# Norm weights applied to turned rows, and the openings of four phases reordered, in a two-layer cross-attention kernel

## The chip, the cores and the metric

The kernel runs as one program on one core of a Trainium2 chip. The metric is device time in microseconds (us); three timed runs of the kernel before had a median of 3099.26 us (3098.64 to 3100.08).

## The reference, cut to what matters

Sixteen sequences of 256 rows with 512 channels pass through two layers; sixteen heads of 32 channels each. The first layer normalises x and the context (each with its own gain and shift), attends under a given mask, adds, and runs an MLP of 2048 hidden channels with GELU. The second layer does a causal self-attention without norm in front, a norm, a cross-attention to the context, a norm (ln2), a small MLP with ReLU, and a last norm.

```
xq  = layer_norm(x, qn_w, qn_b);  ctx = layer_norm(context, cn_w, cn_b)
x   = x + softmax(mask(xq @ q_w, ctx @ k_w)) @ (ctx @ v_w) @ proj_w + proj_b
x   = x + gelu(layer_norm(x, n2_w, n2_b) @ fc1_w + fc1_b) @ fc2_w + fc2_b
x1  = layer_norm(x + mha(x, x, causal), ln1_g, ln1_b)
x2  = layer_norm(x1 + mha(x1, context), ln2_g, ln2_b)
out = layer_norm(x2 + relu(x2 @ f1.T + f1_b) @ f2.T + f2_b, ln3_g, ln3_b)
```

In the second layer each head's keys count only up to a length, which is the number of scores of its row 0 that are not zero, and rows of x that are all zero are masked.

## The kernel before

There are four phases, each with its own buffers, semaphores and a barrier at its end: masked attention (tiles named `mask_`, 0 to 729 us in the trace), the MLP (`mlp_`, 733 to about 1525), causal attention (`causal_`, 1530 to 2150) and cross-attention with the small MLP (`cross_`, 2154 to the end). A phase hands its rows to the next through DRAM. Nothing of a phase starts before the barrier.

Each number is kept as a high part that TensorE takes whole (type fp32r) and a low part, the rest. A product is therefore three matmuls for each block of 128 inputs (`product`, L99): high by high, high by low, low by high. High parts are made by ScalarE (matrix_hi at L462 and L464, `turned` at L470), low parts by VectorE as a difference (matrix_lo at L780, `turned` at L820, `qk_lo` at L830 and L835).

The order of work is written out by hand, engine by engine, in functions `mask_turn`, `causal_turn` and `cross_turn`, one turn for each sequence, 16 turns in a phase; the middle ones run as a hardware loop. In a turn TensorE interleaves, for sequence b, scores (L1279), the turning of exponentials (`turn_probs`, L1300) and products with values (L1319), and, for b+1, the turning of the rows (`turn_over`, L1227) and their products with the matrices. In the cross phase the ln2 norm of sequence b-1 and its MLP lie in the same turn (L1337 turns the normed rows). Engines wait by counted semaphores. In the MLP a turn has 512 rows and 16 steps m; step m is `hidden(m)` and `down(m-1)`, 12 matmuls of 128x512 each, and at the end of a turn TensorE turns the next rows (L2035).

Before its first turn each phase has an opening: rows are loaded by SyncE's DMA queue, matrices of 1 MB each (512x512) arrive through two staging slots, and a slot is loaded again only when both parts of what it held are made. The MLP has eight such pieces, four of W1 and then four of W2; all eight are made before the first rows are normed (`apply`, L1958) and turned.

In the mask phase and in the MLP the norm's gain is folded into the matrix (ScalarE's scale at L462 and L1915), and the norm's shift is sent through the unscaled matrix once as a bias: matmuls with one column, L1205 and L2024, and L1210 for the values. In the cross phase gain and shift of ln2 are applied to the rows before they are turned, by `ln_gain` (L916) and `ln_shift` (L925), two instructions each on VectorE.

## Time and profile before

| | before |
|---|---|
| median of 3 timed runs | 3099.26 us |
| the profiled execution | 3095.5 us, span 3093.7 us |
| mean granted TensorE clock | 0.962 |
| busy: TensorE (PE) | 2857.9 us, 92% |
| busy: VectorE (DVE) | 1759.6 us, 57% |
| busy: ScalarE (ACT) | 1614.8 us, 52% |
| busy: GpSimd (POOL) | 566.5 us, 18% |

Busy time is the time in which an engine had an instruction running. A clock of 1.0 is 2.4 GHz and 0.5 is 1.2 GHz. The profiled execution lies 3.8 us under the median of the timed runs, and its span lies 1.8 us under its own time. In the rows further down, `[25.57 <-DVE mlp_xn L1958]` behind an instruction says that its engine had been idle for 25.57 us until that instruction of VectorE released it; "x8" says that eight were merged in one row.

### The profile page before, as it was taken

The numbers are of one execution on the slowest core, as the hardware profiler recorded it, in microseconds if no ns is written. First come the engines' busy times: TensorE is split into PE (matmuls) and PEld (weight loads), VectorE is DVE, ScalarE is ACT, GpSimd is POOL, SyncE is SP. The second block draws the span as 40 slices with busy tenths as digits, with TensorE's granted clock in tenths as the row PEclk, the third lists the DMA queues.
The fourth block names the chain that finished last, engine by engine and source line by source line (L and its number), as shares of the span: only waits on it lengthen the run. The fifth ranks groups of instructions, "written<-read, shape, count | busy, mean of one in ns | idle before, by whom it ended". The sixth has DMA issues, their size and how long they took to land. (4 is left out here: it accounts for less than half of the span.)

```text
span 3093.7 us, 69198 instructions
## 1 busy us (share of the span) xinstructions
PE 2857.9 (92%) x25032; PEld 2480.7 (80%) x25032; DVE 1759.6 (57%) x5398; ACT 1614.8 (52%) x4889; POOL 566.5 (18%) x709
## 2 busy tenths in 40 slices
PE   7999999996699999999789999995799999999995
PEld 6888888885588888888688888884688888888884
DVE  5666666663333323323267777774576767667674
ACT  4777777773211111111167777775565665656662
POOL 1110111110000000000012222333021313223132
PEclk9999999997799999999899999997899999999997
DMA  2111111113100000000111111112201111100100
GB/s 93 45 56 56 56 49 35 55 42 107 54 28 27 14 14 27 27 27 14 61 36 55 41 41 41 41 41 76 93 28 41 41 41 41 40 34 34 41 28 21
DMA packets 73746, 134.35 MB, mean 43 GB/s; under 512 B 9040, under 2 KB 9040, under 8 KB 73680
## 3 DMA queue, kind: packets, MB, share of 16 engines
q1 hardware_dynamic: 73680, 133.47, 12.6%
q8 instruction: 41, 0.67, 0.1%
q14 instruction: 25, 0.20, 0.0%
HBM read 99.90 MB, written 33.55 MB: 43 GB/s over the span
## 5 line engine op out<-in xcount | busy, mean ns | idle before, releaser
L1926 ACT ACTIVATE mlp_h<-mlp_f,mlp_hb 128x512 f32<-128x512 f32 x128 | 88.3, 690 | 579.8 <-PE mlp_f L99 579.8
L1969 DVE CAST mlp_hT_hi<-mlp_h 128x512 fp32r<-128x512 f32 x128 | 58.1, 454 | 471.6 <-ACT mlp_h L1926 471.6
L888 DVE CUSTOM_DVE_ANT_0 mask_scores<-mask_scores,mask_mask 128x256 f32<-128x256 f32 x512 | 201.6, 457 | 93.8 <-PE mask_scores L1279 93.8
L502 ACT ACTIVATE mask_prob<-mask_scores,mask_low 128x256 f32<-128x256 f32 x512 | 237.4, 476 | 22.5 <-DVE mask_low L888 22.5
L502 ACT ACTIVATE cross_prob<-cross_scores,cross_low 128x256 f32<-128x256 f32 x512 | 238.0, 493 | 6.7 <-DVE cross_low L882 6.7
L502 ACT ACTIVATE causal_prob<-causal_scores,causal_low 128x128 f32<-128x128 f32 (+1 forms) x512 | 211.5, 434 | 13.2 <-DVE causal_low L888 13.1
L99 PE MATMUL mlp_f<-mlp_xT_hi,mlp_w_hi 128*128 128x512 f32 x512 | 200.4, 391 | 1.5 <-DVE mlp_xT_lo L1963 1.5
L99 PE MATMUL mlp_f<-mlp_xT_hi,mlp_w_lo 128*128 128x512 f32 x512 | 200.1, 391 | 0.0
L99 PE MATMUL mlp_f<-mlp_xT_lo,mlp_w_hi 128*128 128x512 f32 x512 | 200.1, 391 | 0.0
L2049 PE MATMUL mlp_acc<-mlp_w_hi,mlp_hT_hi 128*128 128x512 f32 x512 | 199.9, 390 | 0.0
L2049 PE MATMUL mlp_acc<-mlp_w_hi,mlp_hT_lo 128*128 128x512 f32 x512 | 199.3, 389 | 0.0
L2049 PE MATMUL mlp_acc<-mlp_w_lo,mlp_hT_hi 128*128 128x512 f32 x512 | 199.2, 389 | 0.0
L888 DVE CUSTOM_DVE_ANT_0 causal_scores<-causal_scores,causal_tri 128x128 f32<-128x128 f32 (+1 forms) x512 | 164.7, 395 | 30.2 <-PE causal_scores L1285 30.2
L364 POOL TENSOR_SCALAR cross_q<-cross_own_head,cross_qk_parts 128x128 fp32r<-128x128 f32 x128 | 69.2, 552 | 605.5 <-DVE cross_qk_parts L835 605.5
L99 PE MATMUL causal_work<-causal_xT_hi,causal_w_hi 128*128 128x256 f32 x512 | 159.2, 311 | 16.7 <-DVE causal_xT_lo L820 16.7
L882 DVE TENSOR_REDUCE cross_low<-cross_scores 128x2 f32<-128x512 f32 x256 | 160.1, 683 | 18.1 <-PE cross_scores L1285 17.5
L99 PE MATMUL causal_work<-causal_xT_hi,causal_w_lo 128*128 128x256 f32 x512 | 145.5, 284 | 0.0
L99 PE MATMUL causal_work<-causal_xT_lo,causal_w_hi 128*128 128x256 f32 x512 | 145.0, 283 | 0.0
L514 ACT ACTIVATE cross_probT<-cross_probsT 128x512 f32<-128x512 f32 x128 | 76.4, 597 | 128.1 <-PE cross_probsT L1300 128.1
L364 POOL TENSOR_SCALAR causal_q<-causal_own_head,causal_qk_parts 128x128 fp32r<-128x128 f32 x128 | 58.0, 465 | 361.1 <-DVE causal_qk_parts L835 361.1
L99 PEld LDWEIGHTS causal_work<-causal_xT_hi,causal_w_hi 128*128 128x128 f32 x512 | 97.7, 191 | 29.2 <-issue 29.2
L514 ACT ACTIVATE mask_probT<-mask_probsT 128x512 f32<-128x512 f32 x128 | 76.7, 599 | 76.2 <-PE mask_probsT L1300 76.2
(313 smaller groups left out, 9327.3 us busy)
## 6 DMA issues: line engine op xcount, KB each, us to landing
mask_x_in<-in_x SPq DMA_DIRECT2D x16, 512.0 KB, 4.0
mask_c_in<-in_ctx SPq DMA_DIRECT2D x16, 512.0 KB, 5.2
mask_res<-in_x SPq DMA_DIRECT2D x16, 512.0 KB, 3.7
after_attention<-mask_res SPq DMA_DIRECT2D x16, 512.0 KB, 5.9
mlp_x<-after_attention SPq DMA_DIRECT2D x8, 1024.0 KB, 5.6
after_layer<-mlp_y SPq DMA_DIRECT2D x8, 1024.0 KB, 4.2
causal_x_in<-after_layer SPq DMA_DIRECT2D x16, 512.0 KB, 3.6
causal_res<-after_layer SPq DMA_DIRECT2D x16, 512.0 KB, 3.9
```

Of the source, the lines that this page charges most:

```text
L99: last = pe.matmul(out, lhs(k, a), rhs(k, c), start=(k == 0 and n == 0), stop=(k == KC - 1 and n == len(PASSES) - 1))
L364: ins = pool.tensor_scalar(Q0[:, part, :], own_head[:], QK[:, c % 2, 1 - part, 0:1].bitcast(F32), 1.0, ALU.mult, ALU.mult)
L502: ins = act.activation(prob[:, u % 4, qt, 0:w], SC[h][:, FROM[qt]:FROM[qt] + w], ACT.Exp, bias=low[:, u % 4, qt:qt + 1], scale=-1.0, accum ...
L514: act.activation(probT[:, u % 8, 0:n], PT_BANK[u % HC][:, 0:n], ACT.Copy).then_inc(s["copied"], 1)
L882: ins = dve.tensor_reduce(low[:, u % 4, :], SC[h][:].rearrange("p (t k) -> p t k", t=TT), AX_X, ALU.min)
L888: ins = dve.tensor_tensor_reduce(SC[h][:, at], SC[h][:, at], extra, 1.0, F32_MAX, ALU.add, ALU.min, low[:, u % 4, qt:qt + 1])
L1926: act.activation(h32[:, m % 2, :], F1[m % 2][:], ACT.Gelu, bias=hb[:, m:m + 1]).then_inc(s["gelu"], 1)
L1969: dve.tensor_copy(hT[0][:, r, :], h32[:, r, :]).then_inc(s["h_hi"], 1)
L2049: ins = pe.matmul(ACC[t][:], hT[a][:, m % 2, t * P:(t + 1) * P], W2[p][:, m, :], start=(m == 0 and n == 0), stop=(m == MH - 1 and n == 2))
```

## The change

Mask phase: matrices are no longer scaled and no bias is computed. Instead ScalarE applies gain and shift while it copies turned rows out of PSUM, two instructions of 128x256 into a new tile `t32`, and VectorE makes the high part by a copy and the low part by a difference, both from `t32`. The copy of q and k becomes one ScalarE instruction of 512 columns and one VectorE instruction, before two each. The copy of the values moves from VectorE to ScalarE. TensorE waits for ScalarE only (`t_act`) before it writes the bank of scores again.

All three attention phases: the first rows' DMA is followed at once by all matrices, each with its own staging place (in `probT` and `prob`, which are free then); high and low parts are made in the order in which TensorE takes them, and signalled for each block of 128 inputs; `first_product` waits block by block.

MLP: rows first, then pieces alternately from W1 and W2 through two own staging slots; `apply` and the first turning follow the first piece, and the other pieces are made during turn 0. Gain and shift are applied to turned rows as above. In every later turn `turn_over` of the next rows is split: two before `down(14)`, two before `down(15)`.

Causal phase: `front` and `rows_seen`, the scan of the next rows for zeros, move on VectorE from behind `ln_var` to behind `minima(b, 3)`.

Cross phase: `ln_gain` and `ln_shift` become `normed_rows`, two instructions behind `cuts(b, 2)`; the gain goes into the copies of the turned rows (`post_hi`, `post_lo`, two instructions where one was), the shift goes through fc1 once (`shift_through`, 16 matmuls with one column), and GpSimd applies gain and shift to the residual rows (`residual(b)`, four instructions of 128x512 in each turn, behind `query0(b, 3)`).

```diff
@@ ScalarE, attention phases @@
             def turned(b, k):
                 act.wait_ge(s["t_ps"], NP * b + k + 1)
+                if masked_ctx:
+                    if k >= 2 or not isinstance(b, int) or b > 0:
+                        act.wait_ge(s["t_lo"], NP * b + k - 1)
+                    at = 2 * (k // 2)
+                    for i in range(2):
+                        ch = 2 * (k % 2) + i
+                        ins = act.activation(t32[:, k % 2, i, :], T_BANK[k][:, i * S:(i + 1) * S], ACT.Identity,
+                                             scale=wcol[:, at, ch:ch + 1], bias=wcol[:, at + 1, ch:ch + 1])
+                    ins.then_inc(s["t_act"], 1)
+                    return
@@ VectorE, attention phases @@
-                dve.wait_ge(s["w_hi_done"], i + 1)
...
+                for k in range(KC):
+                    dve.wait_ge(s["w_hi_done"], KC * i + k + 1)
...
+                if masked_ctx:
+                    dve.wait_ge(s["t_act"], NP * b + k + 1)
+                    dve.tensor_copy(dst_t[0][:, sl, :], t32[:, k % 2]).then_inc(s["t_hi"], 1)
+                    dve.wait_ge(s["t_hi"], NP * b + k + 1)
+                    dve.tensor_tensor(dst_t[1][:, sl, :], t32[:, k % 2], dst_t[0][:, sl, :].bitcast(F32), ALU.subtract
+                                      ).then_inc(s["t_lo"], 1)
+                    return
@@ GpSimd, cross phase @@
+            def residual(b):
+
+                hold(pool, s["post_ps"], 2 * b, s)
+                for t in range(TT):
+                    pool.tensor_tensor(res[:, t], res[:, t], g_rep[:], ALU.mult).then_inc(s["res_gained"], 1)
+                for t in range(TT):
+                    pool.wait_ge(s["res_gained"], TT * (b - 1) + t + 1)
+                    ins = pool.tensor_tensor(res[:, t], res[:, t], b_rep[:], ALU.add)
+                ins.then_inc(s["res_shifted"], 1)
@@ TensorE, attention phases @@
+            def first_product(out, i, lhs, rhs, t_lo):
+
+                for k in range(KC):
+                    pe.wait_ge(s["w_lo_done"], KC * i + k + 1)
+                    if k % 2 == 0:
+                        pe.wait_ge(s["t_lo"], t_lo + k // 2 + 1)
+                    for n, (a, c) in enumerate(PASSES):
+                        ins = pe.matmul(out, lhs(k, a), rhs(k, c), start=(k == 0 and n == 0),
+                                        stop=(k == KC - 1 and n == len(PASSES) - 1))
+                return ins
@@ VectorE, MLP @@
             norm(0)
-            for i in range(8):
...
             apply(0)
+            matrix_lo(0)
             for k in range(KC):
                 turned(0, k)
-            with dve.Fori(0, TURNS - 1) as b:
+            matrix_lo(1)
+
+            def turn(b, first=False):
                 for m in range(MH):
                     split(b, m)
+                    if first and m < 6:
+                        matrix_lo(m + 2)
@@ TensorE, MLP @@
                 if not last:
-                    for k in range(KC):
-                        turn_over(b + 1, k)
+                    turn_over(b + 1, 0)
+                    turn_over(b + 1, 1)
+                down(b, MH - 2)
+                if not last:
+                    turn_over(b + 1, 2)
+                    turn_over(b + 1, 3)
                 down(b, MH - 1)
```

VectorE in the MLP's opening, before: these rows stand behind six of the eight pieces' low parts, and end with the first turned rows.

```order
L1993 TENSOR_TENSOR mlp_w_lo<-mlp_xn,mlp_w_hi 128x512 x4
L1993 TENSOR_TENSOR mlp_w_lo<-mlp_y,mlp_w_hi 128x512 x4
L1996 TENSOR_TENSOR mlp_hb<-mlp_f_0,mlp_b1col 128x16
L1958 TENSOR_SCALAR mlp_xn<-mlp_x,mlp_mv,mlp_rstd 128x512 x4
L1963 TENSOR_TENSOR mlp_xT_lo<-mlp_turned,mlp_xT_hi 128x512 x4
```

VectorE in the MLP's opening, changed: the rows from the phase's start to the first turned block.

```order
L1995 BN_STATS mlp_stats<-mlp_x 128x6 x4
L1999 BN_AGGR mlp_mv<-mlp_stats 128x2 x4
L2002 TENSOR_SCALAR mlp_rstd<-mlp_mv 128x4
L2007 TENSOR_SCALAR mlp_xn<-mlp_x,mlp_mv,mlp_rstd 128x512 x4
L2013 TENSOR_TENSOR mlp_w_lo<-mlp_stage,mlp_w_hi 128x512 x4
L2019 CAST mlp_xT_hi<-mlp_xT 128x512
L2021 TENSOR_TENSOR mlp_xT_lo<-mlp_xT,mlp_xT_hi 128x512
```

`apply` (L1958, now L2007) stood behind all eight pieces and now stands ahead of the first one's.

VectorE in a causal turn, before: from the scan of the next rows to the attended rows `causal_z`, which TensorE's `turn_over(b+1, 1)` waits for because it writes the same bank.

```order
L809 TENSOR_REDUCE causal_big<-causal_x_in 128x2
L814 TENSOR_SCALAR causal_m_next<-causal_big 128x2
L843 TENSOR_SCALAR causal_flags,causal_lens<-causal_probsT 128x256
L846 TENSOR_SCALAR causal_cut<-causal_key,causal_lens 128x256
L848 RECIPROCAL causal_nan<-causal_lens 128x1
L850 TENSOR_SCALAR causal_nan<-causal_nan 128x1
L896 RECIPROCAL causal_rs<-causal_sums 128x8
L900 TENSOR_TENSOR causal_rs<-causal_rs,causal_m_cur 128x8
L902 TENSOR_TENSOR causal_z<-causal_attended,causal_rs 128x2x128
```

The same place of the changed kernel.

```order
L870 TENSOR_SCALAR causal_flags,causal_lens<-causal_probsT 128x256
L873 TENSOR_SCALAR causal_cut<-causal_key,causal_lens 128x256
L875 RECIPROCAL causal_nan<-causal_lens 128x1
L877 TENSOR_SCALAR causal_nan<-causal_nan 128x1
L911 RECIPROCAL causal_rs<-causal_sums 128x8
L915 TENSOR_TENSOR causal_rs<-causal_rs,causal_m_cur 128x8
L917 TENSOR_TENSOR causal_z<-causal_attended,causal_rs 128x2x128
```

The scan (L809, L814) is gone from this place.

VectorE in a cross turn, before: from `ln_gain` to the cuts. L52 and L827 are register steps, L923 a wait; L843 starts `cuts`.

```order
L916 SCALAR_TENSOR_TENSOR cross_res<-cross_res,cross_mv,cross_g_rep 128x512 x2
L52 REGISTER_ALU
L827 REGISTER_ALU
L835 TENSOR_TENSOR cross_qk_parts<-cross_work,cross_qk_parts 128x2x256
L923 ISA
L925 SCALAR_TENSOR_TENSOR cross_res<-cross_res,cross_rstd,cross_b_rep 128x512 x2
L843 TENSOR_SCALAR cross_flags,cross_lens<-cross_probsT 128x256
L846 TENSOR_SCALAR cross_cut<-cross_key,cross_lens 128x256
L848 RECIPROCAL cross_nan<-cross_lens 128x1
```

The same place of the changed kernel, from the end of `ln_var` to `normed_rows` (L933).

```order
L926 TENSOR_SCALAR cross_minus_mean<-cross_mv 128x2
L927 TENSOR_SCALAR cross_rstd<-cross_mv 128x2
L861 REGISTER_ALU
L862 TENSOR_TENSOR cross_qk_parts<-cross_work,cross_qk_parts 128x2x256
L870 TENSOR_SCALAR cross_flags,cross_lens<-cross_probsT 128x256
L873 TENSOR_SCALAR cross_cut<-cross_key,cross_lens 128x256
L875 RECIPROCAL cross_nan<-cross_lens 128x1
L52 REGISTER_ALU
L877 TENSOR_SCALAR cross_nan<-cross_nan 128x1
L931 ISA
L933 TENSOR_SCALAR cross_res<-cross_res,cross_minus_mean,cross_rstd 128x512 x2
```

`ln_gain` is gone from ahead of `qk_lo` (L835, now L862), and the norm's instructions stand behind the cuts, not ahead of them.

## Rows read from the trace of the kernel before

**Rows 1.** The page, part 2: TensorE's granted clock in 40 equal slices.
```profile
PEclk9999999997799999999899999997899999999997
```

**Rows 2.** Four openings, two cross turns: us, busy of PE, PEld, DVE, ACT, POOL, clock, DMA.
```profile
0.00:47.60 47.60, 31.28 (x160) 27.71 (x160) 21.15 (x44) 14.04 (x23) 5.76 (x12) 0.96 0.40 141
729.00:803.30 74.30, 31.34 (x144) 30.39 (x145) 32.69 (x51) 22.13 (x37) 7.03 (x8) 0.53 0.45 152
1530.00:1565.50 35.50, 13.70 (x87) 13.23 (x87) 11.97 (x24) 8.73 (x16) 3.66 (x13) 0.58 0.40 134
2154.00:2199.80 45.80, 17.90 (x123) 16.64 (x124) 21.93 (x40) 16.43 (x37) 4.63 (x14) 0.59 0.54 190
2360.80:2414.50 53.70, 51.43 (x519) 45.32 (x518) 37.88 (x89) 32.80 (x102) 14.25 (x19) 1.00 0.11 39
2577.60:2632.30 54.70, 52.61 (x519) 46.77 (x518) 37.86 (x89) 32.80 (x102) 14.24 (x19) 0.97 0.10 38
```

**Rows 3.** TensorE's waits over the run: us in total, times, longest.
```profile
PE mlp_turned L2035 <- DVE mlp_xn L1958: 25.6, 1, 25.6
...
PE cross_scores L1227 <- DVE cross_xT_lo L820: 17.8, 1, 17.8
...
PE cross_scores L1279 <- DVE cross_xT_lo L820: 17.5, 14, 1.3
...
PE causal_attended L1227 <- DVE causal_z L902: 13.3, 14, 1.0
...
PE cross_probsT L1300 <- DVE cross_flags L843: 11.7, 14, 1.5
...
PE mlp_turned L2035 <- DVE mlp_xT_lo L1963: 7.4, 8, 1.0
```

**Rows 4.** Timeline of the mask opening: start us, us, engine, line.
```profile
13.49 6.96 PE L1205 MATMUL mask_work<-mask_wcol,mask_stage 128*128 128x1 f32 x32 [13.49 <-DMA mask_stage<-in_L_xattn_q_w]
...
27.62 5.09 PE L1210 MATMUL mask_work<-mask_stage,mask_bias_rep 128*128 128x512 f32 x8
```

**Rows 5.** Timeline of one mask turn, ScalarE.
```profile
235.40 0.47 ACT L481 ACTIVATE mask_qk_parts<-mask_work,mask_qk_bias 128x256 fp32r<-128x256 f32 x1 [0.19 <-PE mask_work L99]
...
243.57 0.60 ACT L470 ACTIVATE mask_cT_hi<-mask_scores 128x512 fp32r<-128x512 f32 x1 [0.79 <-PE mask_scores L1227]
```

**Rows 6.** Timeline of the MLP opening.
```profile
735.12 0.43 SPq L1856 DMA_DIRECT2D mlp_x<-after_attention  x1
...
741.67 2.47 DVE L1946 BATCH_NORM_STATS2 mlp_stats<-mlp_x 128x6 f32<-128x512 f32 x4 [12.45 <-DMA mlp_x<-after_attention]
...
791.41 5.79 DVE L1958 TENSOR_SCALAR mlp_xn<-mlp_x,mlp_mv,mlp_rstd 128x512 f32<-128x512 f32 x4
...
803.32 0.77 PE L99 MATMUL mlp_f<-mlp_xT_hi,mlp_w_hi 128*128 128x512 f32 x1 [1.50 <-DVE mlp_xT_lo L1963]
```

**Rows 7.** VectorE's groups in the MLP, 900 to 1450 us: busy us, mean ns.
```profile
L1969 DVE CAST mlp_hT_hi<-mlp_h 128x512 fp32r<-128x512 f32 x99 | 45.7, 462 | 352.8 <-ACT mlp_h L1926 352.8
...
L1958 DVE TENSOR_SCALAR mlp_xn<-mlp_x,mlp_mv,mlp_rstd 128x512 f32<-128x512 f32 x24 | 11.5, 542 | 0.0
```

**Rows 8.** Timeline of the causal opening, ScalarE.
```profile
1547.67 2.19 ACT L464 ACTIVATE causal_w_hi<-causal_stage 128x512 fp32r<-128x512 f32 x4 [5.17 <-DMA causal_stage<-in_L_xattn_Wv]
```

**Rows 9.** Timeline of the cross opening, ScalarE.
```profile
2172.45 2.19 ACT L464 ACTIVATE cross_w_hi<-cross_stage 128x512 fp32r<-128x512 f32 x4 [4.84 <-DMA cross_stage<-in_L_xattn_Wv]
```

**Rows 10.** Timeline of one cross turn, VectorE and TensorE.
```profile
2569.20 1.00 DVE L900 TENSOR_TENSOR cross_rs<-cross_rs,cross_m_cur 128x8 f32<-128x8 f32 x1
...
2579.21 1.52 DVE L925 SCALAR_TENSOR_TENSOR cross_res<-cross_res,cross_rstd,cross_b_rep 128x512 f32<-128x512 f32 x2
...
2581.69 1.29 DVE L820 TENSOR_TENSOR cross_xT_lo<-cross_scores,cross_xT_hi 128x512 fp32r<-128x512 f32 x2
...
2583.03 0.63 PE L1279 MATMUL cross_scores<-cross_qk_parts 32*128 32x256 f32 x12 [1.25 <-DVE cross_xT_lo L820]
```

**Rows 11.** TensorE in a stretch of that turn: busy (x), clock.
```profile
2583.60:2587.00 3.40, 3.40 (x36) 0.51 0.00 0
```

More of the change, by code:

```diff
@@ L427, in turn @@
                     query0(b, 3)
+                if prev:
+                    residual(b)
                 if nxt:
@@ L551, in mask_turn @@
                     exps(b, 3)
+                    values(b, 1)
                     copy(b, 0)
@@ L594, in mask_turn @@
                     exps(b, 15)
+                if nxt:
+                    values(b + 1, 0)
+                if cur:
                     copy(b, 12)
@@ L997, in mask_turn @@
                     minima(b, 0, (2, 3))
-                    values(b, 1)
                 if prev:
@@ L1141, in cross_turn @@
                     hidden_parts(b, 1)
+                else:
+                    shift_through()
                 if cur:
@@ L1166, in _ @@
             front(0)
-            if lengths:
-                rows_seen()
-            for i in range(min(NM, 3)):
-                matrix_lo(i)
-            for k in range(NP):
-                turned(0, k)
-            for i in range(3, NM):
-                matrix_lo(i)
-            dve.wait_ge(s["vec_loaded"], IT * NV)
-            if lengths:
-                dve.wait_ge(s["pool_setup"], 4 if causal else 2)
-            qk_lo(0, 0)
-            if masked_ctx:
-                values(0, 0)
-                mask_floats(0)
-            else:
+            if masked_ctx:
+                matrix_lo(0)
+                turned(0, 0)
+                turned(0, 1)
+                matrix_lo(1)
+                turned(0, 2)
+                turned(0, 3)
+                matrix_lo(2)
+                qk_lo(0, 0)
+                mask_floats(0)
+                matrix_lo(3)
+            if causal:
+                rows_seen()
+                turned(0, 0)
+                turned(0, 1)
+                for i in range(NM):
+                    matrix_lo(i)
+                dve.wait_ge(s["pool_setup"], 4)
+                qk_lo(0, 0)
                 cuts(0, 0)
                 qk_lo(0, 1)
+            if cross:
+                rows_seen()
+                turned(0, 0)
+                turned(0, 1)
+                matrix_lo(0)
+                turned(0, 2)
+                turned(0, 3)
+                matrix_lo(1)
+                dve.wait_ge(s["pool_setup"], 2)
+                qk_lo(0, 0)
+                cuts(0, 0)
+                matrix_lo(2)
+                qk_lo(0, 1)
+                matrix_lo(3)
+                matrix_lo(4)
+            dve.wait_ge(s["vec_loaded"], IT * NV)
             turn(0, prev=False)
@@ L1726, in cross_turn @@
                     feed1(b, 1)
+                else:
+                    pe.wait_ge(s["v_ready"], 2 * b + 2)
+                    shift_through()
                 if cur:
@@ L2010, in _ @@
                 finish(b)
+            turn(0, first=True)
+            with dve.Fori(1, TURNS - 1) as b:
+                turn(b)
             for m in range(MH):
@@ L2032, in turn_over @@
                 if k >= 2:
-                    pe.wait_ge(s["t_lo"], KC * b + k - 1)
+                    pe.wait_ge(s["t_act"], KC * b + k - 1)
+                elif first is False:
+                    pe.wait_ge(s["t_act"], KC * b)
                 for t in range(NT):
@@ L2036, in turn_over, with hidden, down @@
                 ins.then_inc(s["t_ps"], 1)
-            def hidden(b, m):
-                product(pe, F1[m % 2][:], lambda k, a: W1[a][:, k, m * P:(m + 1) * P],
-                        lambda k, p: xT[p][:, k, :]).then_inc(s["f1_ps"], 1)
-            def down(b, m):
+            def hidden(b, m, first=False):
+                if first and m % 4 == 0:
+                    pe.wait_ge(s["w_lo"], m // 2 + 1)
+                for k in range(KC):
+                    if m == 0:
+                        pe.wait_ge(s["t_lo"], KC * b + k + 1)
+                    for n, (a, p) in enumerate(PASSES):
+                        ins = pe.matmul(F1[m % 2][:], W1[a][:, k, m * P:(m + 1) * P], xT[p][:, k, :],
+                                        start=(k == 0 and n == 0), stop=(k == KC - 1 and n == 2))
+                ins.then_inc(s["f1_ps"], 1)
+            def down(b, m, first=False):
                 pe.wait_ge(s["h_lo"], MH * b + m + 1)
+                if first and m % 4 == 0:
+                    pe.wait_ge(s["w_lo"], m // 2 + 2)
                 for t in range(NT):
```

372 lines of the change are left out of this document (168 added, 204 removed).

## The prediction

> **What bounds the kernel now.** I read the granted clock over the span first [rows 1]: it is full except at four dips, three where a phase ends and the next opens, and one at the end. The openings measured by themselves [rows 2] say the same: in the MLP's opening TensorE is busy for 31.3 of 74.3 us at a mean clock of 0.53, in the causal one for 13.7 of 35.5 us, in the cross one for 17.9 of 45.8 us. The mask opening has 31.3 of 47.6 us, but much of that is bias matmuls. The last two of those rows are single cross turns, 53.7 and 54.7 us long. So TensorE is the bound inside turns, and nothing but what it waits for can be won there; outside, the order of loads and copies is the bound. The list of TensorE's waits gives the prices [rows 3]: 25.6 us for the normed rows of the MLP, 17.8 us in the cross opening, and in turns four repeated waits: 17.5 and 11.7 us in 14 cross turns each, 13.3 us in 14 causal turns, 7.4 us in eight MLP turnings. No repeated wait of the mask phase is among the large ones.
>
> **MLP opening.** Before, rows land at 741.67, but `apply` runs at 791.41, behind eight pieces, and the first `hidden` begins at 803.32 [rows 6]. Now: the rows' DMA, issued at 735.12 behind four vectors, is first. I put it 1.9 us earlier, so they land at 739.8. Statistics take 2.47, and I allow 2 us for the small steps on VectorE and GpSimd (an estimate): `apply` starts at 744.2. It took 5.79 us beside GpSimd's `residual`, and would take 4 x 0.542 = 2.17 us by the steady rows [rows 7]. `residual(0)` can start at the same time again, so I take 5.8: 750.0. Then the first piece's low parts: a difference of 128x512 is 0.65 us (1.29 for two [rows 10]), four are 2.6: 752.6. Then a copy of 0.46 [rows 7] and a difference of 0.65: the first block is ready at 753.7, and each further one takes 1.1 us, while TensorE needs about 1.3 for its three matmuls at half clock. 803.3 - 753.7 = 49.6 us won. Half clock may hold a little longer, 1.6 us: **-48** (bounds -40 and -53; the first if a late vector or piece holds ScalarE, the second if `apply` runs free of GpSimd). Remaining pieces are made inside turn 0: 2.6 us of VectorE in every 5.5 us step of TensorE, of which `split` takes 1.1; a 1 MB piece at 152 GB/s [rows 2] is 7 us, and two are needed in 22 us. That hides, at a cost of nothing; if it did not, two pieces of stall would be 14 us.
>
> A row and a rule meet in `apply`: the four scalings take 5.79 us beside GpSimd's additions and 2.17 us alone [rows 6, 7]. The Trainium skill, "SBUF — State Buffer", section "Who interferes with whom", says that VectorE in a two-port mode and GpSimd take one port pair in turn for whole instructions, so the loser blocks. By it the opening costs what I took, and with no such lock it would be 3.6 us shorter. It speaks against the new `residual(b)` in the cross phase too, which is the last rival.
>
> **Mask opening.** Two runs of 6.96 us and one of 5.09 leave TensorE: 19.0 us [rows 4]. Not all of it comes back. The first matrix was there at 13.49, behind five vectors; now the vectors come behind x, context and two matrices, that is one further MB, at 141 GB/s [rows 2] 7.4 us later, less 2.3 us because they are not ahead: gain and shift at about 18. From there VectorE has the second matrix's low parts, 2.6, and four turned blocks of 1.1: 25. The K product at half clock is some 2.6 us more, and about 6 us of products lie between it and the first scores in either kernel: 33.6, against 47.6: **-14** (bounds -11 and -19).
>
> **Mask turns.** ScalarE's copy of a turned block was 0.60 us; two of 128x256 are 0.84 (0.47 each, partly overlapped [rows 5]). VectorE's 0.65 becomes 1.1. So a turned block is ready 0.7 us later. The keys of b+1 take their third and fourth block right when they are ready: I find 0.24 us of slack on the third and 0.2 on the fourth. What is left is some 0.55 us a turn, in 15 turns **+8** (bounds 0, if the wait for `t_act` that frees the banks sooner gives it back, and +16, if ScalarE, with more work at that place, is late for the exponentials behind it). The copy of q and k is shorter by 0.24 us on ScalarE, and the values' copy moved to it lies in idle time; I take nothing for both.
>
> **MLP turns.** Seven waits of 0.9 us between turnings, out of 7.4 us in eight [rows 3], are covered by `down(14)`: **-7** (bounds -8 and -4).
>
> **Causal opening.** The third matrix began to be copied at 1547.67, after 5.17 us of waiting, because its DMA was issued only when a slot was free [rows 8]. Rows waited behind it. Without it the third matrix follows the second at once, 7 us after the DMA rate of 134 GB/s, and rows are turned first; scores move from 1565.5 to about 1554.5: **-11** (bounds -8 and -12.5).
>
> **Causal turns.** The wait for `causal_z` is 13.3 us in 14 [rows 3]. The scan takes 1.2 us ahead of it on VectorE, more than the wait. At its new place, behind the last minima of the turn's first part, VectorE waits for TensorE anyway, which hides it (without that cover it would cost its 1.2 us a turn, 17 us). SyncE's queue issues the next row load and the store behind it later, with most of a turn left to land: **-13** (bounds -15.5 and -8).
>
> **Cross opening.** As causal: the third matrix waited 4.84 us [rows 9] and rows of x and context stood behind it, 17.8 us of wait for TensorE [rows 3]. By the same steps the first scores come 13 us sooner; `shift_through`, 16 one-column matmuls (the 32 of [rows 4] took 6.96 us at half clock), gives 2 us back: **-11** (bounds -7 and -16).
>
> **Cross turns.** Two waits a turn, 11.7/14 = 0.8 and 17.5/14 = 1.25 us [rows 3]. In the turn shown L925 takes 1.52 and stands ahead of the cuts, the low parts are made from 2581.69, scores begin at 2583.03 [rows 10]. Now `ln_gain` is gone and cuts come first, so the 0.8 vanishes, and the norm takes 2 x 0.54 = 1.1 us: low parts from 2580.9, scores at 2582.25. That is 0.8 us won, not 2.0, since the second wait stays. `post_hi` and `post_lo` become two instructions for one: 0.24 us and 0.3 us on the way to `feed1`: +0.55. Net -0.25 a turn, -3.5. Right behind the two waits the granted clock falls: 0.51 over 3.4 us [rows 11], that is 1.2 GHz, after a stretch in which TensorE stood still twice. A stretch at half clock that did 1.7 us of work at full costs up to 1.7; the turn at 2577.6 has it, with a clock of 0.97, and is 1.0 us longer than the one at 2360.8, whose clock was 1.00 [rows 2]; I count ten such turns. With one wait fewer I expect it gone: -10. Together **-14** (bounds -25, if the post copies hide, and +4, if the clock still falls). The end of the phase I take as unchanged.
>
> **Sum.** -48 - 14 + 8 - 7 - 11 - 13 - 11 - 14 = -110. From the profiled execution's 3095.5 us that gives 2985.5; timed runs lay 3.8 us above it, so 2989 us.
>
> **Rivals.** (1) The clock still falls in the cross turns: +10, 2999 us. For it: the longer wait, 1.25 us, stays. Against: early turns without the fall have the same waits, so it is at an edge. (2) Turn 0 of the MLP starves, or the vectors land late in an opening because DMAs now queue up: +10 to +18, 2999 to 3007. For it: 1 MB takes 7 us. Against: there are 22 us for two. (3) GpSimd's `residual(b)` holds VectorE up. Its four instructions are 5.8 us a turn, by the four beside `apply` [rows 6]; a tiny VectorE product of 128x8 beside such an instruction took 1.00 us [rows 10]. If two VectorE instructions a turn are hit on TensorE's path, that is 1.6 us x 15 = 24, 3013 us. The kernel would be slower than before only from 110/15 = 7.3 us a turn on, more than all four instructions last; so this ends on the other side only if TensorE's clock also stays low for much of each turn. (4) The change only moves waits: the scan and the norm delay what stands behind them by as much; turns then give nothing: 3095.5 - 84 + 8 + 3.8, 3023 us.
>
> **How the numbers follow.** The forecast has 0.6, rival 1 0.17, rival 2 0.1, rival 3 short of slower 0.06, rival 4 0.05, no change 0.01, slower 0.01. The bounds of the terms, taken together as independent, are some 20 us; upward the first three rivals reach 3013. So 2966 to 3012. Under 0.2% (6 us) a measurement could not tell a change: faster 0.98, same 0.01, slower 0.01.
>
> **What would show it.** First `hidden` near 754; first scores near 33.6, 1554.5 and 2182; no wait for `causal_z` and none between MLP turnings; a new wait of TensorE for `mask_cT_lo` of 0.5 us in 15 turns; one wait, not two, in a cross turn and a clock of 1.0 there. Wrong if a cross turn is longer than 54 us, or if a matrix lands late in turn 0.

## The result, and the profile after

The changed kernel took 2970.85 us (median of four runs, 2967.58 to 2974.51), the kernel before 3099.47: a ratio of 0.9586 with a 95% interval of 0.9569 to 0.9602, or 128.6 us less. 2989 us were forecast, with a range of 2966 to 3012.

The page of the changed kernel (span 2965.3 us): busy time of the engines in its first part, and the granted clock in 40 slices. The dip at the MLP's opening, two slices at 7 in [rows 1], is gone; that of the causal phase reads 8 as before, that of the cross phase 7 and 9 for 7 and 8. TensorE was busy for 54 us less, since bias matmuls left and it worked less at half clock.

```profile
PE 2803.9 (95%) x24864; PEld 2430.4 (82%) x24864; DVE 1747.2 (59%) x5357; ACT 1632.9 (55%) x4947; POOL 631.0 (21%) x773
...
PEclk9999999999999999999899999997999999999998
```

Busy time by stretch, the four openings and one cross turn, as in [rows 2] (columns: us, busy PE, PEld, DVE, ACT, POOL, clock, DMA share, GB/s). The openings end here where the first scores, or in the MLP the first hidden step, begin.

```profile
0.00:30.70 30.70, 13.18 (x88) 11.95 (x88) 17.15 (x35) 14.65 (x27) 5.84 (x12) 1.00 0.65 219
727.40:747.00 19.60, 3.91 (x16) 3.08 (x17) 12.42 (x20) 3.78 (x7) 6.88 (x6) 0.50 0.52 176
1463.90:1486.00 22.10, 14.04 (x83) 12.99 (x83) 12.06 (x24) 8.84 (x16) 3.67 (x13) 0.67 0.59 214
2055.00:2080.70 25.70, 14.60 (x71) 13.16 (x71) 13.16 (x26) 9.09 (x17) 4.00 (x12) 0.53 0.92 321
2254.70:2307.50 52.80, 51.17 (x519) 45.26 (x518) 37.23 (x89) 32.96 (x103) 18.21 (x22) 1.00 0.11 40
```

The mask opening lasts 30.7 us where it took 47.6. From the phase's first DMA on, the MLP's takes 19.6 where it took 70.1, the causal one 21.6 for 35.0, the cross one 25.0 for 41.5 (2153.9 to 2195.4 in the trace before). The DMA share rises with it, to 0.92 in the cross opening: matrices now arrive back to back. The clock of the last three openings is still 0.50 to 0.67, so most of the matmuls in them run at 1.2 GHz as before; in the mask opening the clock record begins at 17.4 us, and it is full from there on.

TensorE's waits over the run (us in total, times, longest), with those that answer to [rows 3]:

```profile
PE mlp_turned L2080 <- DVE mlp_xn L2007: 20.1, 1, 20.1
...
PE cross_work L99 <- DVE cross_x2T_lo L962: 13.5, 16, 1.8
...
PE cross_scores L1296 <- DVE cross_xT_lo L854: 11.3, 14, 0.8
...
PE cross_scores L1317 <- ACT cross_prob L519: 3.6, 1, 3.6
```

The waits for `causal_z`, for the cuts and between the MLP's turnings are no longer listed. That for the turned rows' low parts in cross turns fell from 1.25 to 0.8 us, and another has grown beside it: `feed1` waits about 0.8 us for `cross_x2T_lo` in each turn (13.5 us in 16, where the trace before lists 2.3 in 6), since gain is applied there in two instructions.

I measured each phase by the starts of its turns: in the attention phases the first turning of the next rows, in the MLP the turn's first hidden step, because the change moves the first turning ahead of `down(14)`. An opening counts from the phase's first DMA to the start of the second turn, in the cross phase of the third. Against the terms of the forecast:

| part | forecast | measured |
|---|---|---|
| mask opening | -14 | -17.0 |
| mask turns (42.29 to 43.03 us) | +8 | +10.4, and 0.9 at the end |
| MLP opening and first turn | -48 | -52.4 |
| MLP turns (90.19 to 88.86) | -7 | -8.0 |
| causal opening | -11 | -13.3 |
| causal turns (36.05 to 34.73) | -13 | -17.1, and -1.7 at the end |
| cross opening and turn 0 | -11 | -6.8 |
| cross turns (54.3 on average to 52.78) | -14 | -19.7 |
| last cross turn and end | 0 | -3.6 |

Together they are the 128.4 us between the two spans, but for rounding.

Three places of the timeline of the changed kernel carry the differences. The MLP's opening:

```profile
737.56 4.76 DVE L2007 TENSOR_SCALAR mlp_xn<-mlp_x,mlp_mv,mlp_rstd 128x512 f32<-128x512 f32 x4 [1.15 <-POOL mlp_rstd L1933]
...
742.24 3.56 DVE L2013 TENSOR_TENSOR mlp_w_lo<-mlp_stage,mlp_w_hi 128x512 fp32r<-128x512 f32 x4
...
747.01 0.77 PE L2091 MATMUL mlp_f<-mlp_xT_hi,mlp_w_hi 128*128 128x512 f32 x1 [0.55 <-DVE mlp_xT_lo L2021]
```

`apply` takes 4.76 us beside GpSimd's additions, where 5.8 were forecast from [rows 6]; the first hidden step begins at 747.0, 19.6 us after the phase's first DMA. The mask opening:

```profile
14.52 1.93 ACT L486 ACTIVATE mask_t<-mask_scores,mask_wcol 128x256 f32<-128x256 f32 x4 [3.85 <-DMA mask_p_bias<-in_L_xattn_proj_b]
...
17.27 0.45 PE L1395 MATMUL mask_work<-mask_xT_hi,mask_w_hi 128*128 128x256 f32 x1
```

Gain and shift had landed at 14.5, not at 18, and the first product begins at 17.3. The cross phase's turn 0:

```profile
2084.52 2.58 DVE L816 SCALAR_TENSOR_TENSOR cross_w_lo<-cross_probT,cross_w_hi 128x512 fp32r<-128x512 f32 x4
...
2087.03 2.47 DVE L897 TENSOR_REDUCE cross_low<-cross_scores 128x2 f32<-128x512 f32 x4
...
2087.80 0.47 ACT L519 ACTIVATE cross_prob<-cross_scores,cross_low 128x256 f32<-128x256 f32 x1 [2.27 <-DVE cross_low L897]
...
2088.88 0.73 PE L1317 MATMUL cross_scores<-cross_ident,cross_prob 128*128 128x128 f32 x4 [3.58 <-ACT cross_prob L519]
...
2113.23 3.91 PE L1384 MATMUL cross_work<-cross_gb_col,cross_stage 128*128 128x1 f32 x32
```

TensorE waits 3.58 us for the first exponentials. They wait for the minima `cross_low`, which VectorE takes up only after the low parts of the fourth and fifth matrix, 2.58 us each: the first scores begin at 2080.67, their minima at 2087.03, 6.4 us later where it was 1.35 before. ScalarE made the high parts of these matrices as well, but had been idle for 2.27 us when the minima came. `shift_through` takes 3.91 us: its 16 matmuls are recorded as 32, where I had counted 16 records and 2 us.

### The profile page after: what moved, and what is told of

Same layout as the page of the kernel before. It is cut to its first block and busy times, and to the rows that moved or that the text cites. A ratio compares the mean times of both kernels' runs of the same rounds, so it can differ in the third digit from the quotient of the medians.

```text
span 2965.3 us, 69016 instructions
## 1 busy us (share of the span) xinstructions
PE 2803.9 (95%) x24864; PEld 2430.4 (82%) x24864; DVE 1747.2 (59%) x5357; ACT 1632.9 (55%) x4947; POOL 631.0 (21%) x773
## 5 line engine op out<-in xcount | busy, mean ns | idle before, releaser
L1967 ACT ACTIVATE mlp_h<-mlp_f,mlp_b1col 128x512 f32<-128x512 f32 x128 | 88.3, 690 | 559.4 <-PE mlp_f L2091 559.3
L371 POOL TENSOR_SCALAR cross_q<-cross_own_head,cross_qk_parts 128x128 fp32r<-128x128 f32 x128 | 62.0, 497 | 440.1 <-DVE cross_qk_parts L862 430.6
L340 POOL TENSOR_TENSOR mask_rstd<-mask_rstd,mask_half 128x4 f32<-128x4 f32 x16 | 16.8, 1049 | 538.9 <-DVE mask_rstd L834 538.9
```

Source lines behind the costliest of these rows:

```text
L371: ins = pool.tensor_scalar(Q0[:, part, :], own_head[:], QK[:, c % 2, 1 - part, 0:1].bitcast(F32), 1.0, ALU.mult, ALU.mult)
L1967: act.activation(h32[:, m % 2, :], F1[m % 2][:], ACT.Gelu, bias=b1col[:, m:m + 1]).then_inc(s["gelu"], 1)
```

## The experiments

**e1: who makes the mask turn longer?** The copy of the values goes back to VectorE.

```diff
@@ ScalarE, mask_turn @@
-                    values(b, 1)
...
-                if nxt:
-                    values(b + 1, 0)
@@ VectorE, mask_turn @@
                     minima(b, 0, (2, 3))
+                    values(b, 1)
...
                     mask_floats(b + 1)
+                    values(b + 1, 0)
```

> The changed kernel with one part undone: in mask turns VectorE copies the values again, at its old places. Theory (the turned rows' longer chain through ScalarE and VectorE makes a mask turn 0.75 us longer than before): the turn stays at about 43.0 us. Rival (the copies that moved to ScalarE make it late): the turn falls back to about 42.3 us and the kernel to 10 us less than the changed one.

It took 2972.8 us (two runs). One mask turn of it:

```profile
220.80:263.80 43.00, 42.77 (x426) 36.93 (x425) 28.99 (x102) 32.37 (x99) 6.57 (x7) 1.00 0.17 50
```

The turn stays at 43.0 us with ScalarE a microsecond less busy. So the copies that moved cost nothing. The chain through the turned rows reads so in the changed kernel's turn:

```profile
229.37 1.02 ACT L486 ACTIVATE mask_t<-mask_scores,mask_wcol 128x256 f32<-128x256 f32 x2 [0.54 <-PE mask_scores L1244]
...
230.88 0.69 DVE L850 TENSOR_TENSOR mask_cT_lo<-mask_t,mask_cT_hi 128x512 fp32r<-128x512 f32 x1
```

ScalarE's two instructions of one block take 1.02 here, not the 0.84 I had, and the low parts end at 231.6, 2.2 us after ScalarE began. The list of waits shows what comes of it, but in the rows of weight loads (PEld), which stand ahead of the matmuls; the trace before has no such row.

```profile
PEld mask_work L99 <- DVE mask_cT_lo L850: 10.6, 29, 0.8
```

In a middle turn there are two such waits, of 0.32 and 0.38 us, together 0.70 of the 0.74 that the turn grew. With the moved copies out (e1, where the two are the same), the chain is the cause.

**e2: order of norm and cuts in the cross turn.**

```diff
                     qk_lo(b, 3)
-                    cuts(b, 2)
                 if prev:
                     normed_rows(b)
+                if cur:
+                    cuts(b, 2)
```

> The changed kernel with normed_rows ahead of cuts(b, 2) in cross turns, as ln_shift was. Theory (two waits close together bring TensorE's clock down to half, one does not): the wait for the cuts comes back with about 0.8 us, the clock falls to 0.5 after it in most turns, a cross turn takes 53.7 us or more in place of 52.8, so 13 to 25 us in all. Rival (the clock has nothing to do with it, the gain is the removed wait alone): the turn grows by the wait only, up to 0.8 us, with a clock of 1.0, or by nothing if the second wait shrinks by as much.

2973.4 us, and a turn of it:

```profile
2259.60:2312.40 52.80, 51.10 (x519) 45.20 (x517) 37.22 (x88) 32.88 (x103) 18.41 (x22) 1.00 0.11 40
```

The turn is 52.85 us against 52.78 and the clock 1.0. Neither theory was tested, since the wait for the cuts did not come back: without `ln_gain`, cuts are in time in either order. What the order is worth is 0.07 us a turn; what is left as the cause of the missing wait is that 2.9 us of instructions (`ln_gain` 1.41, `ln_shift` 1.52) became 1.0.

**e3: the scan of the causal phase back to its old place.**

```diff
                     ln_var(b, 0)
+                if nxt:
+                    front(b + 1)
+                    rows_seen()
...
                 if nxt:
-                    front(b + 1)
-                    rows_seen()
                     cuts(b + 1, 0)
```

> The changed kernel with front and rows_seen of the causal phase back behind ln_var. Theory (the scan delayed z, which turn_over waits for): the wait for causal_z is back with 0.95 us in each of 14 turns, a turn takes 36.05 us in place of 34.73, 17 to 19 us in all. Rival (the wait was due to something else that the new opening changed): the turn stays at 34.7 us.

2989.8 us, and the wait is back, word for word what it was before:

```profile
PE causal_attended L1245 <- DVE causal_z L917: 13.3, 14, 1.0
```

Its turn is 36.04 us against 34.73. So the move alone is worth 1.31 us a turn, 18 us, while the list of waits puts only 0.95 on it. Most of the rest stands in the list's rows of weight loads, of which [rows 3] has none: there the same wait is 1.19 us.

```profile
PEld causal_attended L1245 <- DVE causal_z L917: 16.6, 14, 1.3
```

**e4: twice the work on GpSimd.**

```diff
                 hold(pool, s["post_ps"], 2 * b, s)
+                for n in range(4):
+                    pool.wait_ge(s["spare_done"], 4 * (b - 1) + n)
+                    pool.tensor_tensor(spare[:], res[:, n % 2], b_rep[:], ALU.add).then_inc(s["spare_done"], 1)
+                pool.wait_ge(s["spare_done"], 4 * b)
```

> The changed kernel with four more GpSimd additions of 128x512 from residual rows into a spare tile at the start of residual(b), so GpSimd works about 10 us there in place of 5. Theory (GpSimd's work beside VectorE costs little, because VectorE's path to TensorE there reads PSUM): a cross turn grows by less than 0.5 us, under 8 us in all. Rival (GpSimd's use of the shared port holds VectorE up on TensorE's path): the turn grows by 1 to 3 us, 15 to 45 us in all.

2973.1 us; the turn is 52.79 us, no longer than before the edit, though VectorE is held up:

```profile
2478.46 5.52 POOL L388 TENSOR_TENSOR cross_spare<-cross_res,cross_b_rep 128x512 f32<-128x512 f32 x4 [5.17 <-PE cross_attended L1359]
...
2485.41 1.45 DVE L991 CAST cross_hT_hi<-cross_h 128x512 fp32r<-128x512 f32 x1 [2.31 <-ACT cross_h L568]
...
2486.89 1.66 DVE L993 TENSOR_TENSOR cross_hT_lo<-cross_h,cross_hT_hi 128x512 fp32r<-128x512 f32 x1
```

GpSimd's additions run until 2489.7, and beside them VectorE's copy takes 1.45 us and its difference 1.66, where the changed kernel shows 0.43 and 0.69. These 2 us end without TensorE waiting longer anywhere: VectorE had been idle for 2.31 us ahead of them. The third rival is out in this place, for a reason of place and not because the two engines don't collide. The Trainium skill says, "SBUF — State Buffer", section "Who interferes with whom", that a VectorE instruction with two inputs in SBUF contends with one of GpSimd that reads SBUF, and that one in a two-port mode blocks or is blocked for a whole instruction. The rows agree for the difference, which has two such inputs, 0.69 us to 1.66; whether the copy ran in a two-port mode they don't show.

**e5 and e6: what brings the clock down?** Two unused scans of 1.2 us are put ahead of the cuts (e5) or behind them (e6), and the norm behind the turned rows.

```diff
                     qk_lo(b, 3)
+                    for n in range(2):                # e5; in e6 behind cuts
+                        dve.wait_ge(s["spare_done"], 2 * b + n)
+                        dve.tensor_reduce(spare[:], x_in[:], AX_X, ALU.max, apply_absolute_value=True
+                                          ).then_inc(s["spare_done"], 1)
                     cuts(b, 2)
-                if prev:
-                    normed_rows(b)
                 if nxt:
                     turned(b + 1, 0)
                     turned(b + 1, 1)
+                if prev:
+                    normed_rows(b)
```

> The changed kernel with two more scans of x_in (1.2 us each, their result unused) on VectorE ahead of cuts(b, 2) in cross turns, and normed_rows moved behind the turned rows, so that TensorE's waits for the cuts and for the low parts stand as far apart and about as long as before. Theory (two waits close together bring the clock down): waits of 0.8 and 1.2 us, the clock at 0.5 for some 3 us after them in most turns, a turn of 54.6 us or more against 52.8. Rival (the lower clock came from something else of the kernel before): the turn grows by the waits alone, 1.0 to 1.5 us, and the clock stays at 1.0.

> As e5, but with the two scans behind cuts(b, 2): the first wait is gone and TensorE stands still once, for about 2 us, at the low parts. If the total idle time counts, the clock falls as in e5 and the turn is as long; if it takes two waits, the clock stays at 1.0 and the turn is about 54 us.

e5 took 3003.8 us, e6 3005.3. TensorE's waits in e5, then two turns of it:

```profile
PE cross_scores L1301 <- DVE cross_xT_lo L855: 18.7, 15, 1.3
...
PE cross_probsT L1322 <- DVE cross_flags L871: 14.0, 16, 1.7
```

```profile
2214.50:2268.80 54.30, 51.38 (x519) 45.27 (x518) 39.48 (x90) 32.98 (x104) 18.17 (x22) 1.00 0.11 39
2268.80:2324.40 55.60, 52.70 (x519) 46.56 (x518) 39.60 (x90) 32.97 (x104) 18.14 (x22) 0.97 0.11 38
```

The same of e6:

```profile
PE cross_scores L1301 <- DVE cross_xT_lo L855: 34.2, 15, 2.3
```

```profile
2266.30:2321.00 54.70, 52.36 (x518) 46.69 (x517) 39.07 (x90) 33.15 (x103) 18.36 (x22) 0.97 0.11 38
2486.50:2540.70 54.20, 51.09 (x518) 45.19 (x517) 39.46 (x90) 32.93 (x104) 18.23 (x22) 1.00 0.11 39
```

In e5 the waits of before are back, in length and distance (0.82 and 1.25 us in a turn, 0.79 and 1.25 before), but not their effect: nine of its 13 middle turns last 54.26 us at full clock and four 55.5 us at 0.97, while in the kernel before nine of 13 have 0.97. "In most turns" was wrong. In e6 TensorE stands still once ahead of the scores, for 2.3 us, and the turns are as long: 54.26 at full clock in five, 54.7 to 55.6 in eight, where the clock is 0.97. In such a turn the clock is at half in one stretch of 3.4 us:

```profile
2218.10:2221.50 3.40, 3.40 (x20) 0.50 0.00 0
```

It begins 5.0 to 6.6 us into the turn, the wait ahead of the scores ends at 5.4. So the clock does come down in some turns when TensorE idles more there, and each time costs 0.4 to 1.3 us: least where it comes last, because there `feed1`'s wait of 0.8 us is gone. That it needs two waits close together is wrong, since one of 2.3 us does it too, and more often. Which turns have it stays open. In e5 they are the first, third, seventh and eleventh of the 13, in e6 the first six, the eighth and the twelfth: the last ones of either run stand four turns apart, though instructions and waits ahead of the scores are the same in every turn. So no run here shows why the kernel before had it so often; what they show is that with the changed kernel's waits of 0.8 and 0.8 us, 5.9 us apart, it came in none of the middle turns.

**e7: the MLP's four turnings in one block again.**

```diff
                     hidden(b, m, first)
-                    if m < MH - 1:
-                        down(b, m - 1, first)
+                    down(b, m - 1, first)
...
-                down(b, MH - 2)
-                if not last:
                     turn_over(b + 1, 2)
```

> The changed kernel with the four turnings of an MLP turn in one block ahead of down(15), as before. Theory: the waits between turnings are back, 1.0 us or, with the longer copies of gain and shift, up to 2 us each turn, and hidden(b+1, 0) may wait for its low parts: a turn of 90.2 us or somewhat more against 88.86, 9 to 20 us in all. Rival (the shorter turn came from the first turn's new order alone): the turn stays at 88.9 us.

2980.1 us, with turns of 89.72 us against 88.86. The third and fourth block's turning:

```profile
1288.06 1.33 PE L2080 MATMUL mlp_turned<-mlp_ident,mlp_xn 128*128 128x128 f32 x8 [0.43 <-ACT mlp_xT L1962]
```

The forecast of 90.2 us or more was too high. The split is worth 0.86 us a turn and not the 1.33 between before and after. The other 0.5 comes from the wait itself: TensorE now waits for ScalarE's copy and no longer for VectorE's low parts before it writes the bank again, so the third block's turning waits 0.43 us where it waited 0.98. `hidden(b+1, 0)` waited for nothing.

**e8: three edits for more.** VectorE takes turned blocks of the mask phase in halves; `feed1` starts with the first half of its inputs; in the MLP's opening `residual(0)` waits until four turned blocks are done.

```diff
@@ VectorE, mask phase @@
-                    dve.wait_ge(s["t_act"], NP * b + k + 1)
-                    dve.tensor_copy(dst_t[0][:, sl, :], t32[:, k % 2]).then_inc(s["t_hi"], 1)
+                    for i in range(2):
+                        at = 2 * (k % 2) + i
+                        dve.wait_ge(s["t_act" if i else "t_first"], NP * b + k + 1)
+                        dve.tensor_copy(dst_t[0][:, at, :], t32[:, k % 2, i]).then_inc(s["t_hi"], 1)
...
@@ TensorE, cross phase @@
-                    pe.wait_ge(s["post_lo"], 2 * b)
-                    feed1(b, 0)
+                    pe.wait_ge(s["post_lo"], 2 * b - 1)
+                    feed1(b, 0, split=True)
@@ GpSimd, MLP @@
+            pool.wait_ge(s["t_lo"], KC)
             residual(0, first=True)
```

> Three edits on the changed kernel: in the mask phase VectorE takes each turned block in halves as ScalarE finishes them; in the cross phase feed1 begins with the first two blocks of the turned rows and waits for the others afterwards; in the MLP's opening GpSimd's residual waits until the first turned rows are done. Theory: the mask turn falls from 43.0 to 42.5 us (7 us), the cross turn from 52.8 to 52.1 (9 us), apply takes 2.2 us and not 4.8 (2.5 us): 18 us less than the changed kernel. Rival (a wait taken away returns at the next step): the turns stay as they are, less than 5 us in all.

2961.5 us (four runs, 2960.3 to 2962.0), 9.4 us less than the changed kernel and half of the 18 expected. Cross turns fell to 52.12 us, as expected. Mask turns fell only to 42.86, 0.17 us and not 0.5. In the MLP `apply` took 1.92 us, and the first hidden step begins 15.6 us after the first DMA and not 19.6. But the first turn behind it, up to the next one's first hidden step, took 96.74 us, 5.7 more:

```profile
747.42 6.34 POOL L1947 TENSOR_TENSOR mlp_y<-mlp_x,mlp_b2r 128x512 f32<-128x512 f32 x4 [8.76 <-DVE mlp_xT_lo L2029]
...
748.13 6.18 DVE L2021 TENSOR_TENSOR mlp_w_lo<-mlp_stage,mlp_w_hi 128x512 fp32r<-128x512 f32 x4 [0.86 <-ACT mlp_w_hi L1962]
...
755.43 0.80 PE L2111 MATMUL mlp_acc<-mlp_w_hi,mlp_hT_hi 128*128 128x512 f32 x1 [4.37 <-DVE mlp_hT_lo L2037]
```

GpSimd now runs beside the second piece's low parts, which take 6.18 us and not 2.5, and TensorE stands still for 4.37 us. The rival was right for this edit: the collision moved to a place where TensorE waits for VectorE, and took more than the 4.0 us won.

**e9: the same with two of them mended.** `residual(0)` waits for the sixth `h_lo`, and in cross turns the normed rows come behind the turned rows, as in e5.

```diff
@@ GpSimd, MLP @@
-            pool.wait_ge(s["t_lo"], KC)
+            pool.wait_ge(s["h_lo"], 6)
             residual(0, first=True)
@@ VectorE, cross_turn @@
                     cuts(b, 2)
-                if prev:
-                    normed_rows(b)
                 if nxt:
                     turned(b + 1, 0)
                     turned(b + 1, 1)
+                if prev:
+                    normed_rows(b)
```

> Four edits on the changed kernel: turned blocks of the mask phase in halves and the split feed1, as in e8; in cross turns the turned rows' low parts ahead of normed_rows; in the MLP's opening GpSimd's residual only after the sixth h_lo, when the pieces are made. Theory: cross turns fall from 52.8 to 51.3 us (20 us), mask turns to 42.85 (2.5 us), the MLP's opening and first turn are 2 us shorter than the changed kernel's: 24 us less than it. Rival (the wait for the low parts comes back at the normed rows' turning, and residual disturbs another place): cross turns stay at 52.1 us, and the MLP's first turn loses again.

2945.4 us (four runs, 2942.3 to 2947.0). Beside it the changed kernel ran again:

> The changed kernel itself once more, timed beside e9 and the others of this call, since its four runs so far lay at 2967.6 to 2968.0 and 2973.7 to 2974.5. If openings differ from run to run by when the clock rises, it lies between 2965 and 2977, and its turns last the same as in the first trace within 0.1 us.

2971.9 us (four runs, 2970.4 to 2976.8), within what was expected, and its turns are those of the first trace within 0.1 us. So e9 is 26.5 us faster than the changed kernel on the same chip, and 0.9517 of the kernel before (0.9501 to 0.9533). The mask opening from 13 to 35 us of e9 and one of its cross turns, then the same opening of e10:

```profile
13.00:35.00 22.00, 18.55 (x121) 17.07 (x122) 14.15 (x33) 11.78 (x23) 1.52 (x3) 0.84 0.39 140
2249.40:2300.60 51.20, 51.15 (x518) 45.24 (x517) 37.09 (x88) 32.94 (x103) 18.23 (x22) 1.00 0.12 41
```

```profile
13.00:35.00 22.00, 18.45 (x139) 17.02 (x140) 15.28 (x36) 13.71 (x31) 1.82 (x3) 1.00 0.40 145
```

No wait of a cross turn is left in the list; the turn is 51.25 us, all of it busy. The MLP's first hidden step comes 15.6 us after the first DMA, against 19.4 in e10, and the turn behind it takes 90.90 us, against 90.91: this time nothing is given back. In the mask opening the clock is 0.84 here and 1.0 in e10, as in the changed kernel's first trace: e9 has a stretch at half clock from 22.6 to 29.4 us. e9's own edit isn't the reason, since e3, e6, e7 and e11, whose mask phase is the changed kernel's, have the same stretch. With it the first scores begin at 32.9 to 33.5 us, without it (the changed kernel twice, e2, e4, e5) at 30.5 to 31.1. What decides between the two stays open. It is the largest part of the few us between runs of one kernel that the traces show; the other openings differ as well, and middle turns at full clock repeat within 0.1 us.

**e11: the later norm alone.** Only the second edit of e9.

> The changed kernel with normed_rows behind the turned rows in cross turns, alone. Theory: low parts are ready 0.9 us earlier, TensorE's wait of 0.8 us is gone and nothing waits for the normed rows, which are turned over a microsecond later: turn 52.0 us, 11 us in all. Rival: the turning of the normed rows waits instead and the turn stays at 52.8 us.

2960.3 us, one turn of it:

```profile
2259.40:2311.30 51.90, 51.08 (x518) 45.25 (x517) 37.06 (x88) 32.94 (x104) 18.17 (x22) 1.00 0.12 40
```

51.9 us against 52.8, and nothing waits for the normed rows: the wait for the low parts is simply gone.

**e12: the changed MLP in the kernel before.**

> The kernel before with the changed MLP phase alone. If the parts add up, it takes what the MLP's opening and turns won together, 57 to 62 us less than before: 3036 to 3042 us. If the changed phases help or hinder each other (a later mask end, a different state of the DMA queue), it lies outside.

3035.9 us, 57.8 less than the kernel before beside it (3093.7). In the table above the MLP's two rows make 60.4, so the phases add up to within 3 us, which openings alone can differ by. The first turning's wait for the normed rows, 25.6 us in [rows 3], is this, counted from the barrier on:

```profile
PE mlp_turned L2039 <- DVE mlp_xn L1966: 20.2, 1, 20.2
```

## Why the prediction was right, and where it was off

The direction, the place of most of the gain and the order of its terms were right. It was 18 us too high, and the measured time lies inside the range, near its low end. What the runs settle by undoing a part are the MLP (e7, e12), the causal turns (e3) and the mask turns (e1). No run undoes the new order in the openings of the attention phases, or parts it from the bias matmuls that left the mask opening; their terms, 37 us together, rest on the traces alone.

**MLP opening: right, 4 us short.** The chain rows, `apply`, low parts, copy and difference came as written: `apply` with 4.8 us for 5.8, the low parts, also beside GpSimd, with 3.6 for 2.6. From the phase's first DMA I had 20.5 us to the first hidden step, and 1.6 for half clock; it was 19.6. The other 1.8 us are turn 0, from its first hidden step to the next turn's: 92.85 us before, 91.06 now. Of these, 1.33 is the split of the turnings at its end, which every turn gains, and the rest fits the clock, which is at half for the turn's first 4.3 us and was for 5.4. The pieces made inside turn 0 cost nothing that shows.

**Mask opening: 3 us short, and its sum is near by luck.** The vectors landed at 14.5, since the queue moved 219 GB/s in this opening and not the 141 of [rows 2] by which I had reckoned, and the clock was full from 17.4 on in that trace, where I had put the K product at half. In e1, with a stretch at half clock, the first scores began at 33.3, beside a forecast of 33.6, but not by its terms: the turned blocks were ready at 22.7 and not 25, then TensorE waited 1.0 us for the values' matrix, which the sum doesn't have, and the products behind it took 8.1 us and not 6.

**Mask turns: right, and by the chain.** +0.74 us a turn for +0.55. ScalarE's pair takes 1.02 us and not 0.84 beside its other instructions; e1 rules out the moved copy. The sign I had named is there, but as two waits of weight loads, 0.70 us together, and not as one of matmuls.

**MLP turns: right, the price low.** 1.33 us a turn for 0.9. e7 parts it: 0.86 is the split, the rest is that a turning waits for ScalarE's copy and no longer for the low parts, which I had left out. The -8.0 of the table are six turns; the seventh stands with the opening.

**Causal opening: right, the size low.** The third matrix no longer waits, and the first scores come 13.4 us sooner, beyond my bound of 12.5. I had reckoned with 134 GB/s; it was 214 ([rows 2] and the rows above).

**Causal turns: the wait was read right, its price too low.** I took the 13.3 us of the list, and e3 shows 18. The upper bound of 15.5 was also too low. The term was mis-sized: I had read the wait in the rows of matmuls, 0.95 us a turn, and the rows of weight loads have 1.19 of the 1.31.

**Cross opening: -11 forecast, -6.8 measured, the one gain that was put too high.** I counted up to the first scores, with 13 us; they come 16.5 us sooner. Behind them I gave 2 us back, and it was 9.6. VectorE makes the fourth and fifth matrix's low parts ahead of the first minima, so that TensorE waits 3.58 us. `shift_through` takes 3.91: I had set its 16 matmuls against the 32 of [rows 4], but those are the records of 16 matmuls too. The last 2 us fit two stretches of 3.4 us at half clock, from 2089.3 and 2116.6, that the trace before doesn't have behind its first scores (an estimate: each can cost up to 1.7). The step that failed is that everything behind the first scores, but for 2 us, would be as before; a matrix that no longer delays the opening delays the turn behind it.

**Cross turns: -14 forecast, -19.7 measured.** The wait for the cuts went, as forecast, and `post_hi` with `post_lo` costs 0.6 us, as forecast with 0.55: `feed1`'s wait in a middle turn grew from 0.2 to 0.8. The wait for low parts fell too, by 0.45 us a turn, since `normed_rows` took 1.0 us in place of 1.5 and started sooner: 0.86 us a turn and not 0.25. And the clock is 1.0 in all middle turns, so the 10 us given back there were there. But my reason for it fell, and the hit is in part luck: e6 has the fall with one wait, e5 with the same two waits as before has it in four turns of 13. The 3.6 us at the end I had put at nothing; the last turn too had waits for the cuts, of 0.79 and 1.45 us, which are gone.

**The rivals.** That the clock still falls did not happen. Late matrices did not happen in the MLP. GpSimd's port: the collision is real (e4, e8) but not on TensorE's path where the change put it. I had priced `residual(b)` with 5.8 us, which is `apply` of VectorE in [rows 6]; its four instructions take 5.0. That the change only moves waits was true of one place, `feed1`, with 13.5 us in 16 turns, and e8 took most of it away again.

## What to carry to other kernels

A phase's opening is worth a timeline of its own: ask in which order TensorE needs what arrives, and have ScalarE and VectorE make it in that order, with the rest inside the first turn; then look at what the moved preparation now stands ahead of. Inside turns, an instruction that nobody waits for soon (a scan, a norm, a residual) belongs behind the last one that TensorE waits for, and e11 got 0.9 us a turn from one such swap. Work on GpSimd is free only where TensorE isn't waiting for VectorE, so its place has to be chosen as carefully as that of VectorE's own.

## What the runs showed of the hardware

A wait that the rows of matmuls put at 0.95 us and those of weight loads at 1.19 gave back 1.31 us a turn when it was removed (e3). Four additions of GpSimd, 6.34 us, lengthened four differences of VectorE beside them from 2.5 to 6.18 us (e8). TensorE's clock came down to half for 3.4 us in some turns of e5 and e6, and stayed full in others whose instructions and waits are the same, at 0.4 to 1.3 us each; the same two waits, of 0.8 and 1.25 us, brought it down in nine of 13 turns of the kernel before and in four of 13 of e5. In the first opening, with the same instructions, it was at half for 6.8 us in some runs and not in others, and the first scores began about 2 us later where it was. Sixteen fp32 matmuls with one column were recorded as 32, and took 3.91 us in the cross phase of the changed kernel and 6.96 in the mask opening of the kernel before.
